# A patch transformer block on one core: one masked softmax normalisation a half, other engines for the keys, a reordered middle and feed-forward, position rows on SP's queue

## The reference, cut to what matters

```python
h = patches(x) @ W.T + b + pos_emb                       # 512 tokens, 768 -> 256
k, q, v = split(layernorm(h) @ W_kqv + b_kqv, 3)
attn = softmax(q @ k.T / 4 + alibi_bias(slopes))          # causal, per image and head, 16 x 16
h = h + (attn @ v) @ W_proj + b_proj

def bitlinear(x, w):                                      # ternary weights with one scale a row
    scale = clip(mean(abs(w), axis=1), 1e-5)
    return x @ (clip(round(w / scale), -1, 1) * scale).T
z = layernorm(h)
a = bitlinear(z, w_fc) + gate * (z @ v.T @ fast_b.T @ u.T)
h = h + bitlinear(relu(a) ** 2, w_proj_mlp)
```

## Time and profile before

| | |
|---|---|
| three runs | 68.31, 70.86, 72.33 us, median 70.86 |
| profiled execution | 68.79 us, of which 67.0 us are the span that the profile shows |
| PE busy | 59.1 us, 88% of the span |
| DVE, ACT, POOL busy | 44.2, 38.8, 27.7 us |
| granted TensorE clock | 1.00 in every slice, its upper level (2.4 GHz) |
| transfers | done at about 19 us, apart from the output |

### The profile page before, as it was taken

The page is one execution under the profiler, slowest core; times in us unless marked ns, Lnnn a source line. Parts: engine busy times, 40 slices in busy tenths (PEclk is TensorE's granted clock), DMA queues, the critical chain, the costliest instruction groups (busy, mean ns, idle before and its releaser), DMA issues.

```text
span 67.0 us, 2165 instructions
## 1 busy us (share of the span) xinstructions
PE 59.1 (88%) x894; PEld 53.3 (80%) x894; DVE 44.2 (66%) x96; ACT 38.8 (58%) x78; POOL 27.7 (41%) x44
## 2 busy tenths in 40 slices
PE   5949999999989999999957969999989999999900
PEld 5918888889968999798936856988969899999800
DVE  0000019657999996999799992723866599989670
ACT  2602001834195969973799699828799358873000
POOL 6500016398788659999956200003900000000700
PEclk9999999999999999999999999999999999999999
DMA  0899999999810000000000000000000000000053
GB/s 1 226 298 296 372 405 404 397 334 370 330 67 0 0 10 0 0 10 0 10 0 0 10 5 5 0 0 10 0 0 0 0 0 0 0 0 0 10 189 124
DMA packets 3371, 6.50 MB, mean 97 GB/s; under 512 B 385, under 2 KB 1314, under 8 KB 3362
## 3 DMA queue, kind: packets, MB, share of 16 engines
q1 hardware_dynamic: 3344, 6.35, 27.1%
q10 hardware_dynamic: 18, 0.03, 0.2%
HBM read 5.85 MB, written 0.52 MB: 95 GB/s over the span
## 4 chain that ended last, share of the span: by engine, by line
PE 57%; DVE 19%; ACT 11%; DMA 5%; issue 4%
PE psum L308 12%; PE psum L497 11%; PE psum L468 9%; DMA pos_sb<-pos 5%; PE psum L374 5%; PE psum L348 5%; PE psum L314 3%; DVE z L792 3%; PE psum L403 3%; PE psum L477 2%; PE psum L328 2%; DVE prob_n L855 2%; DVE bn L784 2%; DVE prob_t L862 2%; PE psum L454 2%
## 5 line engine op out<-in xcount | busy, mean ns | idle before, releaser
L733 ACT ACTIVATE head_sb<-psum,fc_scale 128x256 f32<-128x256 f32 x16 | 6.6, 470 | 3.3 <-PE psum L477 2.7
L497 PE MATMUL psum<-mlp_t,sq_hi 128*128 128x256 f32 x32 | 7.8, 283 | 0.0
L605 ACT ACTIVATE std<-mv,eps_sb 128x1 f32<-128x1 f32 x8 | 2.2, 289 | 9.5 <-DVE mv L786 9.5
L497 PE MATMUL psum<-mlp_t,sq_lo 128*128 128x256 f32 x32 | 7.7, 280 | 0.0
L782 DVE TENSOR_TENSOR h<-psum,posb 128x256 f32<-128x256 f32 x4 | 1.6, 412 | 8.9 <-PE psum L308 8.9
L1072 POOL TENSOR_TENSOR tail_sb<-tail_sb,h 128x256 f32<-128x256 f32 x2 | 1.4, 736 | 13.7 <-DVE tail_sb L891 13.7
L468 PE MATMUL psum<-zt_hi,fc_t 128*128 128x256 f32 x32 | 6.8, 283 | 0.0
L468 PE MATMUL psum<-zt_lo,fc_t 128*128 128x256 f32 x32 | 6.6, 278 | 0.0
L497 PEld LDWEIGHTS psum<-mlp_t,sq_hi 128*128 128x128 f32 x32 | 6.0, 189 | 0.0
L497 PEld LDWEIGHTS psum<-mlp_t,sq_lo 128*128 128x128 f32 x32 | 6.0, 189 | 0.0
L308 PE MATMUL psum<-head_sb,tail_sb 128*128 128x256 f32 x24 | 5.5, 379 | 0.0
(11 more groups left out here) (114 smaller groups left out, 165.6 us busy)
## 6 DMA issues: line engine op xcount, KB each, us to landing
head_sb<-head SPq DMA_DIRECT2D x6, 256.0 KB, 4.7
fc_sb<-w_fc SPq DMA_DIRECT2D x2, 512.0 KB, 6.7
mlp_sb<-w_mlp SPq DMA_DIRECT2D x2, 512.0 KB, 9.3
tail_sb<-tail SPq DMA_DIRECT2D x2, 384.0 KB, 6.1
out<-tail_sb SPq DMA_DIRECT2D x4, 128.0 KB, 1.7
kqv_sb<-w_k SPq DMA_DIRECT2D x1, 256.0 KB, 6.1
kqv_sb<-w_q SPq DMA_DIRECT2D x1, 256.0 KB, 6.1
kqv_sb<-w_v SPq DMA_DIRECT2D x1, 256.0 KB, 5.5
```

The source lines that it names most:

```text
L497: mm = pe.matmul(mlp_ps[f * BH + b], part[:, n % RING, a, b * P:(b + 1) * P], mlp_t[:, 2 * j + a, :], start=j == 0 and a == 0 and i == 0 a ...
L605: nc.scalar.activation(std[:, which, b:b + 1], mv[:, which, b, 1:2], ACT.Sqrt, bias=eps_sb[:, 0:1]).then_inc(std_ready, 1)
L733: nc.scalar.activation(relu[:, n % PART_RING, a, :], FCB[n][:, a * HT:(a + 1) * HT], ACT.Relu, scale=fc_scale[:, 0, m:m + 1]).then_inc(rel ...
```

## The change

It has six parts.

1. The position rows are fetched on SP's queue after the fourth chunk of `head_sb`, not on ACT's queue at the start, and their product comes after the first four chunks of the embedding.
2. The keys of both halves are copied by DVE. Of the four spread copies ACT takes two in half 0 (heads 0 and 3) and DVE one in half 1 (head 3); DVE has none in half 0. DVE makes `zt_lo(1)` after the scales of the first weights.
3. The two divisions of a half, 128x512 each, become a small product `srec_two` (reciprocal times both masks, 128x64) and one product of 128x1024. In half 1 `rows_sum(0)`, which stood between the two divisions, comes after the one.
4. On POOL `residual(1)` moves from before the rounding of the weights to behind it, and `residual(0)` no longer waits for DVE's spread copy.
5. In the middle ACT writes `zt_hi` of the second norm before `duo_rows(1)` and makes `mlp_signs(1)` later, between the steps of the feed-forward; TensorE turns that weight (`turn_mlp(1)`) after `project(1)`. Three PSUM banks of the feed-forward are assigned otherwise.
6. At the end POOL adds h for blocks 0 to 2 and DVE for block 3, and the last block goes out on ACT's queue.

```diff
@@ position rows: SP, TensorE, ACT
             for k in range(KF):
                 sp.dma_start(head_sb[:, k, :], head[:, k, :]).then_inc(head_in[k], 16)
+                if k == POS_FETCH:
+                    sp.dma_start(pos_sb[:, :], pos).then_inc(pos_in, 16)
...
-            pe.wait_ge(pos_in, 16)
-            pe.matmul(pos_ps, pos_sb[:, 0:P], pos_sb[:, P:P + E], start=True, stop=True).then_inc(pos_done, 1)
             for k in range(LAST):
                 pe.wait_ge(head_in[k], 16)
                 for b in range(BH):
                     embed(k, b)
+            pe.wait_ge(pos_in, 16)
+            pe.matmul(pos_ps, pos_sb[:, 0:P], pos_sb[:, P:P + E], start=True, stop=True).then_inc(pos_done, 1)
...
-            act.dma_start(pos_sb[:, :], pos).then_inc(pos_in, 16)
@@ TensorE, middle and feed-forward
             values(1)
+            turn(0, z, z2t_ps[0], z2_ready, z2t_turned)
             pe.wait_ge(mlpt_ready, 1)
-            turn(0, z, z2t_ps[0], z2_ready, z2t_turned)
             spread_scale()
-            pe.wait_ge(duo_ready, 6)
-            turn_mlp(1)
             hidden_main(0, 0, (z2t_hi,))
...
             project(1)
+            turn_mlp(1)
             hidden_low(0, 1)
@@ ACT
-            key_spread(0, (0,))
+            key_spread(0, (0, 3))
...
             mlp_sums(0)
-            key_copy(1)
             exponentials(0)
...
             norm_std(0, 1, var2, std2)
+            norm_std(1, 1, var2, std2)
             mlp_signs(0)
-            norm_std(1, 1, var2, std2)
+            copy_out(z2t_hi[0][:, :, :], z2t_ps[0][:, :], z2t_turned, 1, z2t_hi_ready)
             duo_rows(1)
-            copy_out(z2t_hi[0][:, :, :], z2t_ps[0][:, :], z2t_turned, 1, z2t_hi_ready)
-            mlp_signs(1)
-            copy_out(scale_row[:, :], row_ps, row_done, 1, row_copied)
...
             low_high(0)
+            copy_out(scale_row[:, :], row_ps, row_done, 1, row_copied)
             relus(0)
             squares(0)
             relus(1)
-            squares(1)
             norm_std(2, 1, var2, std2)
             norm_std(3, 1, var2, std2)
+            mlp_signs(1)
+            squares(1)
             relus(2)
+            copy_out(z2t_hi[1][:, :, :], z2t_ps[1][:, :], z2t_turned, 2, z2t_hi_ready)
             relus(3)
-            copy_out(z2t_hi[1][:, :, :], z2t_ps[1][:, :], z2t_turned, 2, z2t_hi_ready)
             squares(2)
...
+            act.wait_ge(out_dve, 1)
+            act.dma_start(out[(BLOCKS - 1) * P:, :], out_sb[:, BLOCKS - 1, :]).then_inc(out_done, 16)
@@ DVE
-            def softmax_divide(f, i):
+            def softmax_divide(f):
                 dve.wait_ge(recip_ready, f + 1)
+                dve.tensor_tensor(srec_two[:, f, :, :], srec[:, f, :].rearrange("p (n o) -> p n o", o=1).broadcast_to(
+                    [P, SCORES, 2]), img_mask.rearrange("p (o i) -> p o i", o=1).broadcast_to([P, SCORES, 2]),
+                    ALU.mult).then_inc(recip_two_ready, 1)
+                dve.wait_ge(recip_two_ready, f + 1)
                 if f > 0:
                     dve.wait_ge(pt_ready, BH * f)
-                dve.scalar_tensor_tensor(prob_n[:, :, i, :], prob[:, f, :, :], img_mask[:, i:i + 1],
-                                         per_row(srec, f), ALU.mult, ALU.mult).then_inc(norm_ready, 1)
+                dve.tensor_tensor(
+                    prob_n[:, :, :, :],
+                    prob[:, f, :, :].rearrange("p n (o s) -> p n o s", o=1).broadcast_to([P, SCORES, 2, S]),
+                    srec_two[:, f, :, :].rearrange("p n (i o) -> p n i o", o=1).broadcast_to([P, SCORES, 2, S]),
+                    ALU.mult).then_inc(norm_ready, 1)
...
-            key_spread(0, (3,))
             fc_sums(0)
-            zt_low(1)
             fc_sums(1)
             scales(fc_sum, fc_scale, 2, E, fc_summed, fc_scaled)
             low_rank_factors()
+            zt_low(1)
             softmax_shift(0)
-            key_spread(1, (3,))
+            key_copy(1)
+            key_spread()
             softmax_sum(0)
...
             softmax_sum(1)
-            softmax_divide(1, 0)
+            softmax_divide(1)
             rows_sum(0)
-            softmax_divide(1, 1)
-            softmax_turn(1)
+            softmax_turn(1, 0)
+            softmax_turn(1, 1)
...
             scale_result(0)
             scale_result(1)
-            for b in (2, 3):
-                scale_result(b)
-                add_result(b)
+            scale_result(2)
+            scale_result(3)
+            add_result(3)
@@ POOL
             key_spread(0, (1, 2))
-            pool.wait_ge(k_spread_dve, 1)
             residual(0)
-            residual(1)
             hidden_factors()
             key_spread(1, (1, 2))
             rounds(fc_sb, fc_scale, fc_whole, range(KH), fc_scaled, fc_rounded)
             rounds(mlp_sb, mlp_scale, mlp_whole, range(KE), mlp_scaled, mlp_rounded)
+            residual(1)
             value_factors()
             for n in SQ_POOL:
                 square(n)
-            for b in range(BH):
+            for b in range(BLOCKS - 1):
                 add_result(b)
```

More of the change, by code:

```diff
@@ L144, in build_program @@
         srec = sb("srec", [P, HALVES, SCORES])
+        srec_two = sb("srec_two", [P, HALVES, SCORES, 2])
         y_duo = sb("y_duo", [P, 2, GRP, BH, PPB, PAIR])
@@ L171, in build_program @@
         mlpt_ps = [psum[:, i:i + 2, :] for i in (2, 6)]
-        z2t_ps = [bank[2], bank[3]]
-        low_ps = [bank[2][:, 0:HT], bank[4][:, 0:HT]]
-        FCB = [bank[i] for i in (0, 1, 2, 0, 5, 1, 2, 0)]
+        z2t_ps = [bank[1], bank[3]]
+        low_ps = [bank[1][:, 0:HT], bank[4][:, 0:HT]]
+        FCB = [bank[i] for i in (0, 2, 1, 0, 5, 1, 2, 0)]
         mlp_ps = [bank[7][:, 0:E], bank[7][:, E:2 * E], bank[3][:, 0:E], bank[6][:, 0:E]]
@@ L272, in build_program @@
         LAST = KF - 2
+        POS_FETCH = 3
         Q, K, V = 0, 1, 2
@@ L294, in _ @@
             sp.dma_start(proj_sb[:, :, :], w_proj).then_inc(proj_in, 16)
-            for b in range(BLOCKS):
-                if b < BH:
-                    sp.wait_ge(out_pool, b + 1)
-                else:
-                    sp.wait_ge(out_dve, b - BH + 1)
+            for b in range(BLOCKS - 1):
+                sp.wait_ge(out_pool, b + 1)
                 sp.dma_start(out[b * P:(b + 1) * P, :], out_sb[:, b, :]).then_inc(out_done, 16)
@@ L363, in scores @@
                 pe.wait_ge(k_spread_act, f + 1)
-                pe.wait_ge(k_spread_dve, f + 1)
+                if f > 0:
+                    pe.wait_ge(k_spread_dve, 1)
                 pe.wait_ge(k_spread_pool, f + 1)
@@ L642, in query_copy @@
                 last.then_inc(q_copied, 1)
-            def key_copy(f):
-                act.wait_ge(k_done, f + 1)
-                for g in range(GRP):
-                    last = nc.scalar.activation(k_sb[:, f, g, :], k_ps[f][:, g * HT:(g + 1) * HT],
-                                                ACT.Identity, bias=k_bias[:, g:g + 1])
-                last.then_inc(k_copied, 1)
             def key_spread(f, heads):
@@ L824, in key_copy, with key_spread @@
                                   ALU.add).then_inc(k_copied, 1)
[L826 to L834 removed]
+            def key_spread():
+                dve.wait_ge(k_copied, 2)
+                src = k_sb[:, 1, :, :].rearrange("p g (n s) -> p (g n) s", s=S)
+                dve.tensor_scalar(k_spread[:, 1, :, 3, :], src, quad_mask[:, 3:4], None,
+                                  ALU.mult).then_inc(k_spread_dve, 1)
             def softmax_shift(f):
```

25 lines of the change are left out of this document (9 added, 16 removed).

## The result

| | before | changed |
|---|---|---|
| executions | 68.31, 68.52, 70.86, 72.33 us, median 69.69 | 70.19, 70.57, 71.40, 73.19 us, median 70.98 |
| profiled execution | 68.79 us, span 67.0 | 71.40 us, span 69.6 |
| PE, DVE, ACT, POOL busy | 59.1, 44.2, 38.8, 27.7 us | 60.7, 45.3, 38.8, 29.0 us |

Changed over before is 1.0246 with an interval of 1.0186 to 1.0307: 2.5% or 1.7 us slower. That ratio compares the quick executions of each kernel; those that the table lists (68.31 and 68.52 against 70.19 and 70.57) lie 2.0 us apart on their means, which is inside the interval. Slower is clear; that it is by more than 2% is not, since the interval begins at 1.86%. The profiled execution of the changed kernel (71.40) is not one of them: its mean granted clock is 0.969, where the two quick ones have 1.00, so its rows carry about 0.8 to 1.2 us more than the 70.19 and 70.57 beside it.

A forecast was written before the change was run, and what follows sets the result against it. TensorE is busy 88% of the span, and the time at which yt of half 0 is ready decides. +1.9 - 0.2 = +1.7 us: 68.8 becomes 70.5, or 69.8 becomes 71.5; forecast's own range 70.6 to 72.6, whole range 69.0 to 73.4.

The forecast's parts named there:

- `yt`: Middle of the attention: yt of half 0, which releases the projection, starts at 36.95 instead of 34.85 us, +2.1.
- first `zt_hi`: Second norm: ACT writes zt_hi at once, not behind duo_rows(1), at 42.5 against 41.40 us, +1.1.
- `hidden_low(0,1)`: Feed-forward: turn_mlp(1) behind project(1) is on TensorE's path, so this goes from 46.71 to 48.4 us, +1.7.
- `low_rank(1)`: Feed-forward: zt_hi(1) is +1.95, the wait there had about 0.1 of slack, so low_rank(1) is +1.9.
- Half 0: Attention, half 0's division and half 1's keys: spread copy +0.40, products behind roundings +0.3; softmax of half 1 starts +0.45.
- rival B: The queue at yt forms but half 0 loses nothing: yt +1.4, sum +1.0, 69.8 or 70.8 us; chance 0.18.
- The queue: Before yt: POOL's residual(1) and DVE's product exclude each other at the port and yt waits for both, +2.1 us.
- Rival A: The product doesn't exclude POOL, or yt goes first: yt +0.25, sum -0.3, 68.5 or 69.5 us; chance 0.25.
- Rival D: The product with two broadcast inputs runs below one column a cycle: about +1.2 each half; with Rival C 0.10.
- Rival C: TensorE idles before project(0) until its clock drops: +1.5 on top, 72 to 73 us; with Rival D 0.10.
- The feed-forward: turn_mlp(1), 0.57 us, falls on TensorE's path; ACT's stretch to zt_hi(1) loses relus (0.84), gains signs (1.12): +0.28.
- The end: Last blocks: DVE skips an addition, -0.35; POOL's addition costs 0.15, two queues 0 to 0.1; taken at -0.2 to 0.

The follow-up runs named there:

- e11_memset: e4_behind plus a POOL memset of 1408 columns behind the rounding, where the changed kernel has residual(1); 1.0054 of the kernel before, from three of twelve executions.
- e4_behind: The changed kernel with residual(1) one call later, behind POOL's value factors; 1.010 of the kernel before, two quickest 69.22 and 69.32 us.
- e10_two_signs: e5_two_divisions with turn_mlp(1) ahead of hidden_low(0, 0) and mlp_signs(1) ahead of the relus; 0.9922 of the kernel before.
- e5_two_divisions: e4_behind with the two divisions of before and yt between them; 0.9994 of the kernel before, three quickest 68.54, 68.69, 68.73 us.
- e1_back: The changed kernel with residual(1) back on POOL ahead of the low-rank factors; 1.019 of the kernel before.
- e6_yt_first: e4_behind with yt of half 0 made ahead of the division of half 1; 1.0061 of the kernel before, quickest 68.98 us.
- e3_warm: The changed kernel with 24 small products without use on TensorE before the projection; 1.0271 of the kernel before.
- e2_late: The kernel before with residual(1) moved behind the rounding and nothing else; 1.0313 of the kernel before.
- e7_pos_only: The kernel before with the position rows on SP's queue and their product behind four chunks; 0.999 of the kernel before.

## Why the prediction was right, and which terms were off

The forecast was +1.7 us, 70.5 in the profile's terms and 71.5 on the middle; measured are +1.7 by the ratio (2.0 between the quick executions listed) and a median of 70.98. The mechanism is as told: POOL's addition of 128x512 and DVE's 1024-column product stand next to each other between 34 and 37 us, one of them longer by 0.99. Of its terms, measured in the profiled execution:

| step | predicted | measured |
|---|---|---|
| start | +0.10 | +0.10 (`h` of block 0 at 9.86, before 9.76) |
| softmax of half 1 starts | +0.46 | -0.02 (30.37 against 30.39) |
| `yt` | +2.1 | +1.78 |
| first `zt_hi` | +1.1 | +2.18 (43.58 against 41.40) |
| first `hidden_low` | +1.1 | +2.17 (47.00 against 44.83) |
| `hidden_low(0,1)` | +1.7 | +2.75 (49.46 against 46.71) |
| `low_rank(1)` | +1.9 | +2.60 (54.79 against 52.19) |
| end | +1.7 | +2.6 (span 69.6 against 67.0) |

From the first `zt_hi` on the measured column holds about 1.3 us of the clock drop, which the predicted one leaves out.

**Half 0, wrong.** I had DVE's spread copy wait for POOL's (+0.40) and both products for roundings (+0.3). DVE was first by 0.06 us and its copy took 0.49; POOL's two took 1.66 instead of the 1.39 that they take in half 0. The product took 1.42 us, 0.20 more than alone: it waited for one rounding, as forecast, but for one only. `srec_two` started at 27.36, 0.17 before the first division of the kernel before, and that paid for it. So half 0 lost nothing, as rival B said.

**The queue, right in kind, its length mis-sized.** B's sum was +1.4, mine +2.1, measured +1.78. (My sum, 34.8 + 1.07 + 1.12, is 36.99 and not 36.95, which changes nothing.) B's start was right and its chain one member short. `srec_two`, with 64 columns, stood in the queue as well: issued at 33.55 it waited for the rounding and ended at 34.47 (0.92 us against 0.29 in half 0), and the addition was next, issued at 34.36. It is recorded as ending at 35.63; taking off the 0.2 us that POOL lets go before its recorded end gives 35.43, and 1.22 us for the product 36.65. The product is recorded as ending at 36.71, and `yt` is issued 0.08 before that. B's sum lacks the 0.29 us of `srec_two`; mine has it, but starts 0.45 too late.

**Rival A is refuted** by the 2.21 us, and by e11_memset's 1.22 beside a fill: the exclusion exists, and it is the reading. **Rival D is refuted**: 1.22 us alone for 1024 columns in e4_behind, where I had 1.21.

**Rival C happened, beside the forecast.** I gave it part of 0.10. In two of the four executions the mean clock is 0.969 and 0.951, in the profiled one the projection takes 3.24 us, +1.27. I had it as a case of its own; it comes on top of the queue and only in part of the executions. The Trainium skill, page "TensorE: Matmul & The Clock Gate", section "Part 1: The HAM clock gate (the "warmup" mystery)", says that an idle TensorE falls to half rate; the clock of 0.50 from 38 us on, behind the wait of 1.98 us, agrees.

**The feed-forward.** The drop passes 1.27 us on to the first `zt_hi`, so without it the row would be at about +0.9 (an estimate) where I had +1.1, which fits `yt`'s missing 0.3. `turn_mlp(1)` then costs 0.58 (2.75 less 2.17), forecast 0.6. ACT's stretch with the signs was forecast at +0.28; from the relu at 49.98 to `zt_hi` at 53.31 it takes 3.33 us, before 3.39: the pair of relus that fell out and the handovers around it were worth as much as the signs. So `low_rank(1)` gave 0.15 back (2.75 to 2.60) instead of losing 0.2 more. e10_two_signs is in line with a gain from the earlier turn, but was not run against e5_two_divisions on one chip.

**The end, wrong by 0.2.** From TensorE's last product to the end of the span it takes 3.37 us in both kernels (66.23 to 69.6, and 63.63 to 67.0). DVE of the changed kernel, then its transfer of the last block:

```profile
65.80 0.90 DVE L888 TENSOR_TENSOR tail_sb<-psum,scale_row 128x256 f32<-128x256 f32 x2 [0.58 <-PE psum L500]
...
66.73 0.64 DVE L892 TENSOR_TENSOR tail_sb<-tail_sb,h 128x256 f32<-128x256 f32 x1
67.40 0.38 ACTq L755 DMA_DIRECT2D out<-tail_sb  x1
```

The gain is there: the chain of waits has the last scaling at 66.27, 0.04 after TensorE, where before it stood at 64.00, 0.37 after. It is spent again. The last addition takes 0.64 us instead of the 0.43 of before, beside POOL's addition of block 2 (another collision at the port, priced at 0.15 and measured at 0.21), and from the end of that addition to the end of the span it is 2.2 us on ACT's queue, 2.1 before. Part 6 was not tried alone.

So the total is right partly by luck, since errors cancel. Up to the first `zt_hi` I was 0.2 too dear and from `hidden_low(0,1)` to `low_rank(1)` 0.35, while the end was 0.2 too cheap. Step by step, with 1.27 us for the drop, the profiled execution would stand at +1.3; with the 0.8 to 1.2 us by which it lies over the quick ones it is +1.4 to +1.8. What fills the distance to the 1.7 us of the ratio is not shown.

## What to carry to other kernels

When two engines share a port, look at what is next in both lists at the moment one of them lets go: a short instruction in such a queue costs the whole of the neighbour's, and a long one was free here where the other engine transposed or had one input in PSUM (in e4_behind the addition of 37.32 ran beside both). Moving an instruction out of one collision is worth trying in each gap of its engine; here the same addition cost 0.6 us in one place (e1_back), 1.0 in the next, and nothing one call later (e4_behind). A ratio from undisturbed executions and the median of all may tell different things, so state which of them a change is for.

## What the runs showed of the hardware that I had not expected

**Very small instructions are held too.** A DVE instruction of 8 columns took 0.82 us instead of 0.17 under POOL's addition (e1_back), one of 64 columns 0.92 instead of 0.29.

**The clock falls after less idle time than the 2.65 us that I had put to rival C, and not always.** In the changed kernel TensorE idled 0.69 and 1.98 us around a product group of 0.61 us before it was at 0.50. In e5_two_divisions the two waits are 0.69 and 0.72 us, and the projection still took 3.53 us:

```profile
34.17 0.61 PE L413 MATMUL psum<-v_sb 16*128 16x16 f32 x4 [0.69 <-ACT y_duo L673]
35.50 3.53 PE L406 MATMUL psum<-proj_sb,yt 128*128 128x256 f32 x8 [0.72 <-DVE yt L860]
```

Which idle stretch decides it is not settled: the kernel before, with waits of nearly that length, shows no drop in its profile, e4_behind with 1.53 us none in its own, and both the wait for `yt` (e6_yt_first) and the fills (e3_warm) were tried.

**TensorE can start at the lower clock, and the clock's row doesn't show it.** In e2_late's profiled execution the first block comes at 12.24 instead of 9.76 us, because the products of the first chunks are slow. Products of the same shape, 128x256 of float32, are the projection's under the granted clock of 0.50 in the changed kernel. Count, then shortest, median and longest in ns, of e2_late from 5.0 to 9.7 us and of the changed kernel from 38.2 to 40.6:

```profile
L308 PE MATMUL psum<-head_sb x10: 631/634/797, 5.3 to 9.3; 128*128 128x256 f32 x10
```

```profile
L406 PE MATMUL psum<-proj_sb,yt x6: 600/634/634, 38.0 to 40.1; 128*128 128x256 f32 x6
```

The median is the same 634 ns, where it is 379 ns at the upper clock, and the products of e2_late fall to 379 ns from 10.0 us on. So the first stretch ran at the lower level, though the page gives the clock as 1.00 there: a clock row of 1.00 at the start is no proof. Of the 11 executions of before beside e7_pos_only, 9 took 71.0 to 72.3 us with a mean clock of 0.99 to 1.00, which fits this start; of the six with part 1, none took more than 70.87 and the median was 69.31 against 71.26.

Part 1 doesn't keep the slow products away. Of the twelve profiled kernels that have part 1, nine show between one and seven of them at the start, for instance e3_warm:

```profile
L310 PE MATMUL psum<-head_sb x6: 634/634/796, 3.5 to 5.8; 128*128 128x256 f32 x6
```

But there they begin at 3.5 to 4.0 us and are over by 6.9 at the latest, and the first block comes at 10.66 us at the latest, not at 12.24. With part 1 TensorE goes on to data 0.0 to 0.5 us after the small products with which it starts; in e2_late it idles 0.7 us before the position rows. So moving these rows, worth nothing at the quick end, seems to make the slow start short and to hide part of it. No profile of a slow start with part 1 undone and done on one chip was taken, so this is inferred from times and from profiles of different kernels.
